# Graph network layer with residual and norm: edge rows fetched in pairs, edge items placed between dense items

## The chip, the cores and the metric

The kernel runs on one core of a Trainium2 chip. The metric is the device time of one execution in microseconds (us). The core has five instruction streams that run in parallel and meet through semaphores: TensorE (PE, with its weight loads listed apart as PEld), VectorE (DVE), ScalarE (ACT), GpSimd (POOL) and SyncE (SP). SP and POOL also issue the DMAs here.

## What is computed

```python
edge_sum = segment_sum(edge_attr, src, num_segments=50000)   # 12500 edges, 128 features
h = elu(concat([x, edge_sum], axis=1) @ W0 + b0)             # x: 50000 x 128, W0: 256 x 128
h = elu(h @ W2 + b2)
out = h @ W3 + b3
result = layernorm(x + out)                                  # over the 128 features
```

All is float32. 12,500 edges name at most 12,500 source rows (11,090 different ones for this input), so most of the 50,000 rows have an edge sum of zero.

## The kernel before

**Dense items.** The 50,000 rows are cut into 98 dense items of 512 rows. A dense item computes its rows as if their edge sum were zero and stores them to `out`. **Edge items.** The edges are sorted by source on the chip (a bitonic network in steps 1 to 19, on DVE with turns on PE). Then 25 edge items of 500 sorted edges each recompute, with the edge sums, the rows that have edges, and scatter them over the dense results in `out`; a last item of 100 rows does the ends of the 100 columns of sorted edges. An edge's row that is not the last one of its source is sent out of bounds and is not written. A scatter must land after the dense store of the same row.

**Steps.** All engines run a software pipeline over steps `c`. In step `c`, PE does `layer1(c-1)`, `turn(c)` for an edge item, `layer2(c-2)` and `layer3(c-3)`, in this order. ACT does `exp(c-1)`, `turned(c)` (x to `xT`), `exp(c-2)`, then `squares(c-3)` with the logarithm and exponential that seed the inverse root. DVE does `root(c-4)`, the first `elu(c-1)`, `normalise(c-4)`, the second `elu(c-2)`. So `h1(c-1)` and `h2(c-2)`, which DVE makes in step `c`, are read by PE in step `c+1`. Each layer's product of 512 columns is two instructions in the trace (they show as x2), and `layer3` is eight pairs of 128 columns.

**The order of items.** Items 0 to 97 are dense, 98 to 122 are the edge items, 123 is `LAST`.

**Edge sums.** For edge group `g`, DVE makes four masks (`masks`, L788) that compare keys, PE multiplies the gathered features by them into `sum_ps` (`sums`, L463), ACT copies the result to `sumT` (`copy_sums`, L574), DVE keeps the edges of it (`keep_parts`, L797), and `layer1` of the edge item adds `w0e` times `sumT` (L498). The step of group `g`'s sums is 95+g. `copy_sums` stands behind `squares` in ACT's step, and the first sum of the next group waits for it (`sum_ready`). At step `END_AT` = 121, `end_sums` puts a short chain PE, DVE, PE, DVE in front of the step.

**Fused bias.** `fused(s, layer)` chooses how the bias gets into a layer. Unfused, DVE uses two instructions for an elu (L819, then L822). Fused, PE adds the bias with a small bf16 product (`add_bias`, L479) and DVE needs one instruction (L815). Steps 3 to 19 are fused in both layers; from step 20 on, only layer 2, and only in even steps of dense items.

**GpSimd.** After the sort it issues, for each group, four gathers of feature rows (L369) and four of x rows (L375), of 125 rows each, paced by `o_ready`; then it waits for all dense stores and issues the 100 scatters (L391) and the last one (L384). Each indirect DMA of 125 rows is one POOL instruction, whose descriptors the engine makes itself.

**SyncE.** In step `c` it issues the load of item `c+3` (L310, 256 KB) and the store of item `c-4` (L317, 256 KB), in order on one queue, and waits for `o_ready` before each store.

## Time and profile before

| | us |
|---|---|
| median of 3 runs | 605.97 (605.18 to 607.83) |
| the profiled execution, its own time | 606.39 |
| its span, first to last instruction | 604.3 |
| PE busy | 544.3 (90%) |
| DVE busy | 466.1 (77%) |
| ACT busy | 439.7 (73%) |
| POOL busy | 371.9 (62%) |

The time of the execution is 2.1 us above the span. The span falls into stages: some 14 us of set-up, the sort with dense items (to step 20, near 101 us), dense items with gathers (to some 400 us), edge items (to some 585 us) and a tail of scatters. An item's steps can be told apart in the timeline by the product of `layer1` (L487), with which each step of PE begins. A timeline row gives start and duration; "x2" merges two instructions; the brackets give the idle time of the engine before it and what ended it. DMA shares are of the core's 16 DMA engines.

### The profile page before, as it was taken

To read this page: it belongs to the slowest core of one execution; us is meant where nothing else is said; L and a number is where in the kernel's file an instruction comes from. 1 tells how busy PE (TensorE), PEld (TensorE's weight loads), DVE (VectorE), ACT (ScalarE), POOL (GpSimd) and SP (SyncE) were. 2 spreads that over 40 slices of the span, in tenths; PEclk is the share of its full clock that TensorE was granted. 3 is DMA by queue.
4 is the path that set the end of the run, shared out by engine and by line. 5 is a ranking of instruction groups with operands and counts; after the bars stand their busy time and mean duration, and the time that the engine had idled before them with its cause. 6 is when DMAs were issued, how large, how long until landed. Compare 5 with 4: busy or idle time off the path is not lost.

```text
span 604.3 us, 10977 instructions
## 1 busy us (share of the span) xinstructions
PE 544.3 (90%) x2930; PEld 360.4 (60%) x2930; DVE 466.1 (77%) x1348; ACT 439.7 (73%) x1632; POOL 371.9 (62%) x310
## 2 busy tenths in 40 slices
PE   3999999999999999999999999989999999997930
PEld 1455555566666666666666666666667666665620
DVE  5988899988888888888888888877678676776640
ACT  2577767888888888888888988876665666665630
POOL 0000000377887787788778778877157777777676
PEclk9999999999999999999999999999999999999985
DMA  3134332486666655555665656554422332211111
GB/s 111 49 109 120 121 106 91 144 245 184 183 180 183 180 175 179 178 174 175 181 180 183 175 174 179 173 153 117 112 77 76 82 79 71 71 38 37 34 39 34
DMA packets 57451, 77.84 MB, mean 129 GB/s; under 512 B 22590, under 2 KB 27782, under 8 KB 57390
## 3 DMA queue, kind: packets, MB, share of 16 engines
q1 hardware_dynamic: 33294, 58.26, 31.7%
q0 software_dynamic: 24096, 18.89, 12.7%
q8 instruction: 24, 0.39, 0.3%
q14 instruction: 37, 0.30, 0.2%
HBM read 45.30 MB, written 32.24 MB: 128 GB/s over the span
## 4 chain that ended last, share of the span: by engine, by line
PE 82%; DVE 9%; issue 5%; POOL 2%; ACT 1%; SPq 0%; DMA 0%; DVEq 0%; POOLq 0%
PE z_ps L531 18%; PE z_ps L532 17%; PE l_ps L519 17%; PE l_ps L487 16%; PE sum_ps L463 5%; PE l_ps L498 4%; PE l_ps L479 3%; PE turn_ps L512 2%; POOL out_dram L391 2%; DVE h L815 2%; DVE net L721 2%; DVE o_sb L850 1%; DVE net L720 1%; PE turn_ps L435 1%; DVE e L819 0%
## 5 line engine op out<-in xcount | busy, mean ns | idle before, releaser
L369 POOL DMA_INDIRECT attr_edge<-in_edge_attr_dram,edge_i x100 | 124.8, 1248 | 143.9 <-issue 141.1
L531 PE MATMUL z_ps<-center,xT 128*128 128x128 f32 (+1 forms) x986 | 194.7, 279 | 8.5 <-issue 6.4
L600 ACT ACTIVATE sq<-z_ps 128x128 f32<-128x128 f32 (+1 forms) x493 | 129.8, 278 | 94.7 <-PE z_ps L532 93.7
L532 PE MATMUL z_ps<-w3c,h 128*128 128x128 f32 (+1 forms) x986 | 190.1, 274 | 0.0
L531 PEld LDWEIGHTS z_ps<-center,xT 128*128 128x128 f32 (+1 forms) x986 | 152.3, 191 | 41.5 <-issue 36.3
L391 POOL DMA_INDIRECT out_dram<-o_sb,target_i x100 | 119.9, 1199 | 53.5 <-issue 49.3
L532 PEld LDWEIGHTS z_ps<-w3c,h 128*128 128x128 f32 (+1 forms) x986 | 149.0, 191 | 0.0
L375 POOL DMA_INDIRECT x_edge<-in_x_dram,key_i x100 | 124.3, 1243 | 30.5 <-issue 28.1
L822 DVE SCALAR_TENSOR_TENSOR h<-l_ps,neg_bias,e 128x512 f32<-128x512 f32 (+2 forms) x174 | 129.2, 742 | 6.2
L519 PE MATMUL l_ps<-h,w 128*128 128x512 f32 (+1 forms) x248 | 130.0, 606 | 1.8 <-DVE h L822 1.8
L591 ACT ACTIVATE e<-l_ps,bias 128x512 f32<-128x512 f32 (+2 forms) x174 | 116.7, 671 | 18.7 <-issue 5.3
L487 PE MATMUL l_ps<-xT,w0x 128*128 128x512 f32 (+1 forms) x248 | 128.8, 601 | 1.2 <-ACT xT L585 1.2
L600 ACT ACTIVATION_READ_ACCUMULATOR sq<-z_ps 128x1 f32 (+1 forms) x493 | 102.0, 207 | 0.0
L819 DVE TENSOR_SCALAR e<-e,bias 128x512 f32<-128x512 f32 (+2 forms) x174 | 95.6, 550 | 3.8 <-issue 2.5
L850 DVE TENSOR_TENSOR o_sb<-z_ps,rstd 128x512 f32<-128x512 f32 (+1 forms) x124 | 84.1, 678 | 0.1
L585 ACT ACTIVATE xT<-x_sb,bias_x 128x512 f32<-128x512 f32 x98 | 69.8, 712 | 7.6 <-DVE neg_bias L668 7.6
L519 PEld LDWEIGHTS l_ps<-h,w 128*128 128x128 f32 x248 | 43.7, 192 | 44.1 <-issue 29.8
L463 PEld LDWEIGHTS sum_ps<-same,attr_edge 125*128 125x128 f32 x200 | 31.8, 190 | 42.9 <-issue 41.7
L832 DVE SCALAR_TENSOR_TENSOR newton<-seed 128x4 f32<-128x4 f32 (+1 forms) x124 | 20.7, 167 | 45.1 <-ACT seed L607 44.3
L591 ACT ACTIVATE e<-l_ps,minus_one 128x512 f32<-128x512 f32 x74 | 49.9, 675 | 4.4 <-PE l_ps L479 3.8
L463 PE MATMUL sum_ps<-same,attr_edge 125*128 125x125 f32 x200 | 39.9, 283 | 12.7 <-issue 12.7
L815 DVE SCALAR_TENSOR_TENSOR h<-e,l_ps 128x512 f32<-128x512 f32 x74 | 50.2, 679 | 0.0
(126 smaller groups left out, 402.5 us busy)
## 6 DMA issues: line engine op xcount, KB each, us to landing
x_sb<-x_items_dram SPq DMA_DIRECT2D x98, 256.0 KB
out_dram<-o_sb SPq DMA_DIRECT2D x98, 256.0 KB
keyB<-key_rows_dram SPq DMA_DIRECT2D x25, 250.0 KB
attr_edge<-in_edge_attr_dram,edge_i POOLq DMA_INDIRECT x100
x_edge<-in_x_dram,key_i POOLq DMA_INDIRECT x100
out_dram<-o_sb,target_i POOLq DMA_INDIRECT x100
w<-in_L_gnn_W_dram SPq DMA_DIRECT2D x2, 64.0 KB, 1.9
w0x<-in_L_gnn_W_dram SPq DMA_DIRECT2D x1, 64.0 KB, 2.1
```

The source lines that it names most:

```text
L369: nc.gpsimd.indirect_dma_start(out=attr_edge[0:EP, c, :], out_offset=None, in_=attr[:, :], in_offset=bass.IndirectOffsetOnAxis(ap=edge_i[0 ...
L375: nc.gpsimd.indirect_dma_start(out=x_edge[0:EP, c, :], out_offset=None, in_=x[:, :], in_offset=bass.IndirectOffsetOnAxis(ap=key_i[0:EP, c: ...
L391: nc.gpsimd.indirect_dma_start(out=out[:, :], out_offset=bass.IndirectOffsetOnAxis(ap=target_i[0:EP, col:col + 1], axis=0), in_=o_sb[0:EP, ...
L463: T.matmul(sum_ps[:, j * EP:(j + 1) * EP], attr_edge[0:EP, c, :], same[0:EP, c % (2 * J), :], start=True, stop=True).then_inc(same_free, 1)
L487: mm = T.matmul(ps, w0x[:], xT[:, c % SLOTS, 0:n], start=True, stop=alone)
L519: mm = T.matmul(l2_ps[c % 2][:, 0:n], w2[:], h1[:, c % 2, 0:n], start=True, stop=not fused(s, 2))
L531: T.matmul(z, xT[:, c % SLOTS, j * q:(j + 1) * q], center[:], start=True, stop=False)
L532: mm = T.matmul(z, h2[:, c % 2, j * q:(j + 1) * q], w3c[:], start=False, stop=True)
L591: A.activation(e[:, c % 2, 0:n], ps[:, 0:n], ACT.Exp, bias=bias[:, 0:1]).then_inc(done, 1)
L600: t = A.activation(sq[0:q, j, :], z_ps[c % 2][0:q, j * P:(j + 1) * P], ACT.Square, scale=float(P) ** -0.5, accum_out=ssq[0:q, c % 2, j:j + 1])
L819: V.tensor_scalar(e[:, c % 2, 0:n], e[:, c % 2, 0:n], 1.0, bias[:, 0:1], ALU.min, ALU.add).then_inc(min_ready, 1)
L822: V.scalar_tensor_tensor(out=h[:, c % 2, 0:n], in0=ps[:, 0:n], scalar=neg_bias[:, 0:1], in1=e[:, c % 2, 0:n], op0=ALU.max, op1=ALU.add).th ...
```

## The change

It has five parts.

1. **Pairs.** A new DRAM tensor `pairs` has a row for each edge: 128 features of its source's x row, 128 edge features. GpSimd fetches x rows by unsorted `src` from the start (100 indirect DMAs, `fetch_x`), SP writes them to `pairs` (25 times `pair_x`, 250 KB, in steps 2 + 3g//2) and copies the features beside them, DRAM to DRAM (25 times `pair_attr`, 256 KB in 512-byte runs, steps 2 to 26). The 200 gathers of 512-byte rows become 100 of 1,024-byte rows.
2. **Order of items.** 50 dense items come first, then edge item, dense, dense, and so on; edge item `g` is item 50+3g, the last is 122. Its sums are in the step before it (49+3g) instead of three steps before. `END_AT` is 123.
3. **Scatter.** DVE derives from the sorted keys how many dense items must be out before group `g` may be scattered (`dense_need`); SP counts landed stores in `dense_out` (`confirm`), and GpSimd waits for that number, read to a register. The scattered rows are written to `pair_edge` instead of `o_sb`.
4. **Sums and their copy.** The four sums stand in two pairs instead of four places, and `copy_sums` stands ahead of `squares`.
5. **Fused bias.** Only steps 3 to 19 are fused; the 40 even steps later are not.

```diff
+    DENSE_BETWEEN = 2
+    ITEMS = [("dense", d) for d in range(ND - DENSE_BETWEEN * (NE - 1))]
+    for g in range(NE):
+        ITEMS.append(("edge", g))
+        if g < NE - 1:
+            ITEMS += [("dense", len(ITEMS) - g - 1 + n) for n in range(DENSE_BETWEEN)]
+    LAST = len(ITEMS)
...
-    SUM_LEAD = 3
-    SUMS = {ND - SUM_LEAD + g: g for g in range(NE)}
+    PAIR_X = {2 + 3 * g // 2: g for g in range(NE)}
+    PAIR_ATTR = {2 + g: g for g in range(NE)}
+    SUM_LEAD = 1
+    SUMS = {EDGE_AT[g] - SUM_LEAD: g for g in range(NE)}
...
         def fused(s, layer):
-            if s < KEY_AT:
-                return FUSED_FROM <= s
-            return layer == 2 and s % 2 == 0 and is_dense(s - 2)
+            return FUSED_FROM <= s < KEY_AT
...
+            def confirm(d):
+                sp.wait_ge(stored[d % SLOTS], 16 * (d // SLOTS + 1))
+                sp.sem_inc(dense_out, 1)
+            def pair_x(g):
+                k = g % SLOTS
+                sp.wait_ge(x_fetched[k], 16 * J * (g // SLOTS + 1))
+                sp.dma_start(pairs.rearrange("(p c) f -> p c f", p=EP)[:, J * g:J * g + J, 0:P],
+                             x_early[0:EP, k, :, :]).then_inc(x_paired[k], 16)
+            def pair_attr(g):
+                last = min(E, ROWS * (g + 1))
+                sp.dma_start(pairs[ROWS * g:last, P:2 * P], attr[ROWS * g:last, :]).then_inc(attr_paired, 16)
...
+                if item_in(c - 4) and is_dense(c - 4):
+                    d = ITEMS[c - 4][1]
+                    store(d)
+                    if d >= 2:
+                        confirm(d - 2)
+                if c in PAIR_ATTR:
+                    pair_attr(PAIR_ATTR[c])
+                if c in PAIR_X:
+                    pair_x(PAIR_X[c])
...
+            def fetch_x(g):
+                k = g % SLOTS
+                at_least(pool, x_paired[k], 16 * (g // SLOTS))
+                for j in range(J):
+                    nc.gpsimd.indirect_dma_start(
+                        out=x_early[0:EP, k, j, :], out_offset=None, in_=x[:, :],
+                        in_offset=bass.IndirectOffsetOnAxis(ap=src_i[0:EP, J * g + j:J * g + j + 1], axis=0),
+                    ).then_inc(x_fetched[k], 16)
...
+            def scatter_out(g):
+                need = pool.value_load(dense_need[0:1, g:g + 1], min_val=2, max_val=ND)
+                pool.wait_ge(o_ready, EDGE_AT[g] + 1)
+                pool.wait_ge(dense_out, need)
...
+            pool.wait_ge(attr_paired, 16 * NE)
             pool.wait_ge(edge_ready, 1)
             for g in range(NE):
                 gather(g)
...
             pool.wait_ge(target_ready, 1)
-            for k in range(SLOTS):
-                pool.wait_ge(stored[k], 16 * DENSE_ON[k])
...
-                return [one(j) for j in range(J)]
+                return [some(0), some(1)]
...
+                if c in SUMS:
+                    parts.append(lambda: copy_sums(SUMS[c]))
                 if item_in(c - 3):
                     parts.append(lambda: squares(c - 3))
                 run(parts, [])
-                if c in SUMS:
-                    copy_sums(SUMS[c])
...
+                link(V.tensor_copy(dense_need[0:1, :], ends[0:1, J - 1:EC:J]))
+                link(V.tensor_scalar(dense_need[0:1, :], dense_need[0:1, :], ROW_BITS, None, ALU.logical_shift_right))
+                V.tensor_scalar(dense_need[0:1, :], dense_need[0:1, :], 2, ND, ALU.add, ALU.min).then_inc(ends_ready, 1)
```

On PE, two dense steps that follow each other in the stage of dense items. `l_ps<-xT,w0x` is layer 1, `l_ps<-h,w` layer 2, `l_ps<-ones_row,bias_rows` the bias product, `z_ps` layer 3. Before:

```order
L487 MATMUL l_ps<-xT,w0x 128x512
L519 MATMUL l_ps<-h,w 128x512
L479 MATMUL l_ps<-ones_row,bias_rows 128x512
L531 MATMUL z_ps<-center,xT 128x128
L532 MATMUL z_ps<-w3c,h 128x128
...
L487 MATMUL l_ps<-xT,w0x 128x512
L519 MATMUL l_ps<-h,w 128x512
L531 MATMUL z_ps<-center,xT 128x128
L532 MATMUL z_ps<-w3c,h 128x128
```

In the changed kernel:

```order
L524 MATMUL l_ps<-xT,w0x 128x512
L556 MATMUL l_ps<-h,w 128x512
L568 MATMUL z_ps<-center,xT 128x128
L569 MATMUL z_ps<-w3c,h 128x128
...
L524 MATMUL l_ps<-xT,w0x 128x512
L556 MATMUL l_ps<-h,w 128x512
```

The bias product of every second step is gone; nothing else of a dense step moved.

On PE, an edge step of before with the sums (`sum_ps`) of a later group in it:

```order
L487 MATMUL l_ps<-xT,w0x 128x500
L498 MATMUL l_ps<-sumT,w0e 128x500
L463 MATMUL sum_ps<-same,attr_edge 128x125
L512 MATMUL turn_ps<-ident,x_edge 128x125 x4
L463 MATMUL sum_ps<-same,attr_edge 128x125
L519 MATMUL l_ps<-h,w 128x500
L463 MATMUL sum_ps<-same,attr_edge 128x125
L531 MATMUL z_ps<-center,xT 125x128
```

In the changed kernel the same work is spread over three steps: the step of the sums, that of the turn and that of the edge item's first layer.

```order
L524 MATMUL l_ps<-xT,w0x 128x512
L500 MATMUL sum_ps<-same,pair_edge 128x125 x2
L556 MATMUL l_ps<-h,w 128x500
L500 MATMUL sum_ps<-same,pair_edge 128x125 x2
...
L524 MATMUL l_ps<-xT,w0x 128x512
L549 MATMUL turn_ps<-ident,pair_edge 128x125 x4
L556 MATMUL l_ps<-h,w 128x512
...
L524 MATMUL l_ps<-xT,w0x 128x500
L535 MATMUL l_ps<-sumT,w0e 128x500
```

The sums now come once in three steps, and two steps lie between them and the product with `w0e`.

On ACT, the copy of the sums. Before, then in the changed kernel:

```order
L591 ACTIVATE e<-l_ps,bias 128x500
L600 ACTIVATE sq,ssq<-z_ps 125x128 x4
L605 ACTIVATE seed<-ssq,eps 125x4
L607 ACTIVATE seed<-seed 125x4
L574 COPY sumT<-sum_ps 128x500
```

```order
L629 ACTIVATE e<-l_ps,bias 128x500
L611 COPY sumT<-sum_ps 128x500
L638 ACTIVATE sq,ssq<-z_ps 128x128 x4
L643 ACTIVATE seed<-ssq,eps 128x4
```

The copy moved from behind the squares of layer 3's result to ahead of them.

## Rows read from the trace of the kernel before

**Rows 1.** Windows view: stretch, then busy us and count of PE, PEld, DVE, ACT, POOL, clock, DMA.

```profile
126.00:390.00 264.00, 258.13 (x1397) 173.37 (x1396) 219.40 (x510) 232.18 (x885) 212.24 (x170) 1.00 0.62 183
```

**Rows 2.** Timeline of two dense steps: start us, us, engine, line, operation, count, [idle <-releaser].

```profile
200.40 1.02 PE L487 MATMUL l_ps<-xT,w0x 128*128 128x512 f32 x2
...
200.60 0.28 ACT L600 ACTIVATE sq<-z_ps 128x128 f32<-128x128 f32 x1 [0.79 <-PE z_ps L532]
...
202.34 0.16 DVE L832 SCALAR_TENSOR_TENSOR newton<-seed 128x4 f32<-128x4 f32 x1 [1.05 <-ACT seed L607]
...
202.92 0.73 DVE L819 TENSOR_SCALAR e<-e,bias 128x512 f32<-128x512 f32 x1
...
203.90 1.02 PE L487 MATMUL l_ps<-xT,w0x 128*128 128x512 f32 x2
...
204.95 0.48 DVE L819 TENSOR_SCALAR e<-e,bias 128x512 f32<-128x512 f32 x1
...
205.46 0.75 DVE L822 SCALAR_TENSOR_TENSOR h<-l_ps,neg_bias,e 128x512 f32<-128x512 f32 x1
...
205.71 0.39 PE L479 MATMUL l_ps<-ones_row,bias_rows 3*128 3x512 bf16 x1
...
206.27 0.49 PE L531 MATMUL z_ps<-center,xT 128*128 128x128 f32 x2 [0.17 <-issue]
...
208.16 1.02 PE L487 MATMUL l_ps<-xT,w0x 128*128 128x512 f32 x2
```

**Rows 3.** Timeline of two edge steps, the first with the sums of a later group.

```profile
474.33 1.01 PE L487 MATMUL l_ps<-xT,w0x 128*128 128x500 f32 x2
...
475.93 0.56 ACT L574 COPY sumT<-sum_ps 128x500 f32<-128x500 f32 x1
...
476.59 0.46 PE L463 MATMUL sum_ps<-same,attr_edge 125*128 125x125 f32 x2 [0.41 <-issue]
...
480.56 1.01 PE L487 MATMUL l_ps<-xT,w0x 128*128 128x500 f32 x2
...
563.96 1.00 PE L487 MATMUL l_ps<-xT,w0x 128*128 128x500 f32 x2
...
568.66 1.00 PE L487 MATMUL l_ps<-xT,w0x 128*128 128x500 f32 x2
```

**Rows 4.** Groups by line and form (busy us, mean ns of one | idle before), and line L834 alone.

```profile
L375 POOL DMA_INDIRECT x_edge<-in_x_dram,key_i x100 | 124.3, 1243 | 30.5 <-issue 28.1 <-DVE o_sb L850 2.4
...
L788 DVE TENSOR_SCALAR same<-keyB,key 125x125 f32<-125x125 f32 x100 | 36.5, 365 | 0.0
...
L834 DVE SCALAR_TENSOR_TENSOR newton<-ssq,newton x124: 159/162/165, 27.2 to 584.3; 128x4 f32<-128x4 f32 x98, 125x4 f32<-125x4 f32 x25, 100x1 f32<-100x1 f32 x1
```

**Rows 5.** DMA: windows of the sort and of the fullest stretch, and the page's two queues.

```profile
30.00:60.00 30.00, 29.53 (x142) 16.11 (x140) 25.07 (x102) 22.26 (x89) 0.00 (x0) 1.00 0.36 111
...
130.00:134.00 4.00, 4.00 (x27) 3.04 (x27) 2.82 (x8) 3.29 (x14) 3.08 (x4) 1.00 1.08 331
...
q1 hardware_dynamic: 33294, 58.26, 31.7%
...
q0 software_dynamic: 24096, 18.89, 12.7%
```

**Rows 6.** Timeline: L487 of step 26, the steps around the end sums, and the tail.

```profile
126.36 1.02 PE L487 MATMUL l_ps<-xT,w0x 128*128 128x512 f32 x2
...
549.36 1.01 PE L487 MATMUL l_ps<-xT,w0x 128*128 128x500 f32 x2
...
557.56 1.03 PE L487 MATMUL l_ps<-xT,w0x 128*128 128x500 f32 x2
...
583.55 0.69 DVE L850 TENSOR_TENSOR o_sb<-z_ps,rstd 125x512 f32<-125x512 f32 x1
...
585.05 1.19 POOL L391 DMA_INDIRECT out_dram<-o_sb,target_i  x1 [0.30 <-DVE o_sb L850]
...
599.98 0.99 POOL L384 DMA_INDIRECT out_dram<-o_sb,end_i  x1 [0.30 <-issue]
```

More of the change, by code:

```diff
@@ L51, in gnn_resnorm @@
     AHEAD = 3
+    DENSE_BETWEEN = 2
[5 more added lines that the diff above has]
+    LAST = len(ITEMS)
+    ITEMS.append(("last", 0))
+    NI = len(ITEMS)
+    DENSE_AT = [c for c in range(NI) if ITEMS[c][0] == "dense"]
+    EDGE_AT = [c for c in range(NI) if ITEMS[c][0] == "edge"]
+    assert [ITEMS[c][1] for c in DENSE_AT] == list(range(ND)) and [ITEMS[c][1] for c in EDGE_AT] == list(range(NE))
     LOG = 7
@@ L260, in blocks @@
             return 1 if c == LAST else J
-        def scatters(c):
-            return 16 * sum(blocks(k) for k in range(ND, c + 1) if k % SLOTS == c % SLOTS)
         def rows(c):
@@ L396, in _ @@
+                        in_=pair_edge[0:EP, c, 0:P], in_offset=None, bounds_check=N - 1, oob_is_err=False,
+                    ).then_inc(scattered, 16)
+            pool.wait_ge(src_loaded, 16)
+            for g in range(NE):
+                fetch_x(g)
+            for k in range(SLOTS):
+                pool.wait_ge(x_paired[k], 16 * len(range(k, NE, SLOTS)))
+            pool.wait_ge(attr_paired, 16 * NE)
             pool.wait_ge(edge_ready, 1)
```

155 lines of the change are left out of this document (72 added, 83 removed).

## The prediction

> **What bounds the kernel now.** I read the windows first, then the timeline step by step, since shares of busy time hide what a step waits for. In the stage of dense items with gathers PE is busy 258 of 264 us, at full clock [rows 1], so PE seems to be the bound and each removed product seems to be worth its length. The timeline says otherwise. Steps begin at 200.40, 203.90 and 208.16: an unfused one of 3.50 us and a fused one of 4.26, 7.76 for two [rows 2]. 3.50 is what PE needs: 2,048 columns (512 for each of two layers, 1,024 in layer 3), or 1.71 ns a column. In the fused step, layer 3 starts at 206.27. The bias product in front of it started at 205.71 and its row ends at 206.10, before that. What ended last was DVE's second elu: 205.46 + 0.75 = 206.21 [rows 2]. So this stage is bound by a loop over two steps: PE ends layer 3 of an item and starts the next step (200.40); ACT, which waits for that, starts the squares at 200.60; DVE starts the root at 202.34, then elu, normalise, elu, and hands over h2 at 206.21; PE starts layer 3 at 206.27 and ends it at 208.16. 0.25 us in it is a DVE instruction that lasted 0.73 instead of 0.48 [rows 2], while GpSimd was making descriptors.
>
> An edge step with sums takes 6.23 us (474.33 to 480.56), one without 4.70 (563.96 to 568.66) [rows 3]. The sums are 4 x 125 columns in float32, 500 x 1.71 ns = 0.86 us. That leaves 0.67 that is no work. ACT's copy of the sums runs from 475.93 to 476.49 and the next group's first sum starts at 476.59 [rows 3]: PE waited for the copy, which stands behind the squares.
>
> At the end, the last edge item is normalised at 583.55 + 0.69 = 584.24, but GpSimd is behind: it issues one scatter in 1.49 us (ten between 585.05 and 599.98) and ends at 600.97, 3.3 us before the end of the span [rows 6].
>
> **Removing the bias products (40 fused steps to none).** By the loop this gives nothing of itself: the unfused step's chain is what both steps wait for, and now every step has it. Two steps take 7.76 - 0.25 = 7.51 without the DVE delay (3.75 each), 7.76 with it in each (3.88). DVE's own work, 202.34 to 206.21 less the 0.25, is about 3.55 a step and fits. The lower bound is PE's 3.50, if ACT or DVE can run ahead, which no row shows; the upper is 3.95, with both elus delayed in some steps. The known delay row is the nearest, but GpSimd's place in the step will drift, so I take two thirds of the delay: 3.83, against 3.88 before. A saving of 40 x 0.76 = 30 us, which the fused step's length suggests, is not there in the dense stage.
>
> **The order of items and the copy of the sums.** From step 49 on, three steps make a cycle: two dense items and one edge item. PE's work is 2 x 3.50 + 4.70 + 0.86 = 12.56 us, in steps of about 4.36 (sums), 3.90 (turn) and 4.30 (product with w0e). Now look at the loop: with the DVE chain of 7.51 over two steps, plus 0.6 for three masks (0.2 each from start to start) where they stand, every two steps here take PE 8.2 to 8.7 us. So in the cycle PE is the bound, the chain is covered, and the fused steps' absence is free. The cover is thin: DVE has 3 x 3.55 + 4 x 0.28 to 0.37 (the masks' mean is 0.365 [rows 4]) + 0.2 = 12.0 to 12.3 of 12.56. The copy is now ahead of the squares, and two steps lie between it and the next sum, so the 0.67 goes; ACT has slack for 0.5 us in a step of 4.3. I take 12.7 a cycle, bounds 12.56 and 13.1. The same three items took 7.76 + 6.23 = 13.99 before: 1.3 saved, 24 times, 31 us.
>
> **Pairs.** GpSimd issues 300 indirect DMAs as before, 1.24 + 0.30 us each [rows 4], but 100 of them from about 3 us on, when it was idle. On SP, `pair_x(g)` waits for a fetch that lands near 12 + 6.2g; SP comes to it near 14 + 7.1g in the sort, and loads and stores queued behind it don't wait. After step 20 SP asks every 5.7 us, but the fetches are up to four groups (25 us) ahead. `pair_x(24)` is in step 38, near 178 us; the gathers then run from 180 to 334, group 0 there by 190 when its sums are due near 216, and each later one 6.2 us after the last, while 12.7 are given. What GpSimd does for `target` and the keys is not touched. The DMA engines are the narrow place. Loads and stores take a share of 0.36 at 111 GB/s in the sort, 0.52 MB in a step of 4.72 us, 1.70 us of all engines [rows 5]. GpSimd's queue moved 18.89 MB in 12.7% of 604.3 us, 4.06 us a MB [rows 5]; at that price three fetches (0.20 MB) are 0.80, two thirds of a `pair_x` 0.68, a `pair_attr` 1.06. The sum is 4.24 of 4.72: it fits, barely. The keys' short DMAs at steps 20 to 24 stand behind such a copy; together with three more DVE instructions I give them 1.0 us (0 to 3).
>
> The Trainium skill (DMA: Bandwidth & Descriptors, Specifications) gives a limit of about 358 GB/s of HBM traffic a core; with both sides of the copy counted this comes to (0.52 + 0.20 + 0.17 + 2 x 0.26) MB in 4.72 us, 299 GB/s, so by that page, as an estimate, it also fits; the fullest stretch of the trace showed 331 GB/s [rows 5].
>
> **Scatters.** They begin at 334 us with some eight items waiting and use 6 us of each cycle's 12.7, so GpSimd is level by about 430. Sources are uniform, so group g needs about 3.9(g+1)+2 dense items, and 50+2g stand before it: only the last two groups wait, group 23 for about a step, group 24 for the last store. Those waits have only scatters behind them.
>
> **The sum, in the trace's own time.** Step 26 begins at 126.4 [rows 6] + 1.0 = 127.4. 23 dense steps x 3.83 = 88.1: 215.5. 24 cycles x 12.7 = 304.8: 520.3. Step 121: 4.36. Step 122: 3.90, and then the end sums, which cost 557.56 - 549.36 - 4.70 = 3.50 [rows 6]: 532.1 for the step of the last edge item's first layer. From there to its normalised rows it was 584.24 - 568.66 = 15.6 [rows 3, 6]; the step behind the end sums was longer by 563.96 - 557.56 - 4.70 = 1.7 [rows 3, 6], and now lies in this stretch: 549.4. GpSimd is level: 0.6 to start, four scatters of 1.49, the last of 0.99, 3.33 to the end: 560.3. Plus 2.1 outside the span, 562.4; the profiled execution stands 0.4 above the median of 605.97: **562.0 us**. Against before, that is 31 in the cycles, 10 in the tail, and little elsewhere.
>
> **The rivals.**
> (a) DVE becomes the bound of the cycle. For: 12.0 to 12.3 of 12.56, and a delay of 0.25 on each of six elus would make 13.5 to 13.8. Against: in steady steps only one in three was delayed. Price 0.5 to 1.1 a cycle: 574 to 588. Chance 0.17.
> (b) The copies hold the sort back. If DRAM to DRAM costs both sides, `pair_attr` is 2.1 and the step needs 5.3 of 4.72: 24 x 0.6 = 14 us, 576. Chance 0.10.
> (c) Slower than before: small packets cost by the piece. SP's queue took 31.7% x 604.3 x 16 / 33,294 = 92 ns a packet, GpSimd's 51 [rows 5]. `pair_attr` and two thirds of `pair_x` put 53 packets of 512 bytes on each engine in a step. At 92 ns a step needs 1.7 + 0.8 + 4.9 = 7.4 us, 24 times 2.7 more: 627. It decides from 76 ns on, where the step takes 1.8 more and the 44 us are gone. GpSimd's rows of 512 bytes speak against it. Chance 0.06.
> (d) The sort's DVE instructions are held by GpSimd, which used to be idle there. Against: L834, with two inputs in SBUF, lasts 165 ns at most in 124 [rows 4], and GpSimd issues DMAs during about 100 of these steps. At 0.3 us for a dozen in each of 15 steps it would cost 54 us: 616. Chance 0.01. The Trainium skill (SBUF — State Buffer, Who interferes with whom) says a VectorE instruction with two SBUF inputs contends with a GpSimd one that reads SBUF; by that rule (d) would come, and the row speaks against it for these DMAs.
> (e) The dense steps run at PE's 3.50: 23 x 0.33 = 8 us less, 554. Chance 0.08.
> (f) The scatters are not level at the end, because `dense_out` comes late: the old tail stays, 572. Chance 0.04.
>
> **How the numbers follow.** The forecast has 0.54, with its own range of 555 to 570 (3.75 to 3.95 a dense step, 12.56 to 13.0 a cycle). 552 to 584 takes in (e), (b), (f) and most of (a), and leaves out (c), (d) and some of the ends, under 0.2. 0.5% is 3 us, about what a measurement can tell here. Faster 0.91, within 0.5% 0.02, slower 0.07.
>
> **What would show it.** Dense steps 26 to 48 at 3.75 to 3.90 with layer 3 behind DVE's elu, not at 3.50; a cycle near 12.7 with PE without gaps; no wait of a sum for the copy; a sort at 4.7 a step; the last scatters within 8 us of the last normalise. Wrong if the DMA share stays at 1 in the sort, or DVE is busy without a gap in the cycle.

## The result, and the profile after

| | before | changed |
|---|---|---|
| median of 20 runs, us | 605.86 (603.84 to 607.87) | 601.5 (591.97 to 605.21) |
| profiled execution, us | 606.39 | 601.51 |
| its span, us | 604.3 | 599.7 |

The ratio changed to before is 0.9837, 95% interval 0.9811 to 0.9863. The forecast was 562.0, with a range of 552 to 584: wrong by 39.5 us. The ratio is taken over each kernel's runs within 1.5% of its fastest, which are 7 of the changed kernel's 20, so it lies under the ratio of the two medians (0.9928). Before's runs lie within 4 us of each other, the changed kernel's within 13. That spread was the first sign that something stood in it that is not in the program.

The engines' busy times and the slices of the page after:

```profile
span 599.7 us, 11136 instructions
PE 534.1 (89%) x2890; PEld 363.3 (61%) x2890; DVE 492.7 (82%) x1391; ACT 434.4 (72%) x1632; POOL 371.2 (62%) x310
PE   3899999779999999999899988788999999999980
ACT  2477775758888888786777774657788887888841
POOL 7766658466672778877887777785444333344306
PEclk9999999989999999999999999989999999999986
```

A slice is 15 us. PE is not full in slices 24 to 28, about 345 to 420 us, at a granted clock of 9 tenths or more but for one slice. The windows view gives the same by stages (stretch, length, then busy us and count of PE, PEld, DVE, ACT, POOL, clock, DMA share, GB/s):

```profile
135.00:224.00 89.00, 83.47 (x459) 57.03 (x458) 80.29 (x185) 78.05 (x299) 57.33 (x46) 1.00 0.76 227
229.00:343.00 114.00, 109.36 (x622) 78.19 (x621) 97.94 (x240) 88.06 (x333) 91.55 (x74) 1.00 0.66 183
343.00:410.00 67.00, 54.45 (x279) 36.25 (x279) 46.13 (x112) 39.99 (x148) 53.49 (x45) 0.97 0.43 118
432.00:560.00 128.00, 127.36 (x749) 93.47 (x749) 113.37 (x293) 106.95 (x401) 48.38 (x40) 1.00 0.38 112
```

From 432 us on PE is busy 127.36 of 128, as forecast for the whole stage. Between 343 and 410 it is busy 54.45 of 67, and so is no one else: DVE 46, ACT 40. DMA has only a share of 0.43 there. GpSimd issues indirect DMAs without a break (45 rows in 67 us): the last gathers, and from 352 us on scatters. The clock explains little: 0.97 instead of 1.00 over 54.45 us of PE's work is some 1.6 us (an estimate from this row).

For the sum I took the start of layer 1 of single items, the rows of L524, item c being in step c+1 (item 25 is the step 26 of the prediction):

```
start of layer 1, us       item 19   item 25   item 48   item 72   item 84   item 96   item 120   end of span
forecast                      -        127.4     215.5      -         -         -       520.3       560.3
changed kernel              101.7      134.6     224.2     333.8     402.6     458.8    560.1       599.7
before                      100.7      126.4       -         -         -         -        -         604.3
```

The 39.4 us that the span is over the forecast are 7.2 up to item 25, 1.5 in the dense steps (89.6 against 88.1), 31.1 in the 24 cycles (335.9 against 304.8) and -0.4 in the tail (39.6 against 40.0). The cycles are not evenly slow: the last eight take 101.3 us, 12.66 each, the forecast's 12.7. The four from item 72 to 84 take 68.8, 17.2 each.

**One slow step, row by row.** The timeline of the changed kernel at 361 to 369 us, ACT first, then PE and GpSimd (start us, us, engine, line, operation, count, [idle before <- releaser]):

```profile
363.51 0.66 ACT L629 ACTIVATE e<-l_ps,bias 128x500 f32<-128x500 f32 x1
364.07 0.71 ACT L623 ACTIVATE xT<-x_sb,bias_x 128x512 f32<-128x512 f32 x1
364.69 0.67 ACT L629 ACTIVATE e<-l_ps,bias 128x512 f32<-128x512 f32 x1
367.92 0.28 ACT L638 ACTIVATE sq<-z_ps 128x128 f32<-128x128 f32 x1 [2.56 <-remote]
...
363.04 0.39 PE L569 MATMUL z_ps<-w3c,h 128*128 128x128 f32 x2
364.84 1.12 PE L524 MATMUL l_ps<-xT,w0x 128*128 128x512 f32 x2 [1.41 <-issue]
...
364.28 1.19 POOL L418 DMA_INDIRECT out_dram<-pair_edge,target_i  x1 [0.30 <-issue]
365.77 1.19 POOL L418 DMA_INDIRECT out_dram<-pair_edge,target_i  x1 [0.30 <-issue]
367.27 1.19 POOL L418 DMA_INDIRECT out_dram<-pair_edge,target_i  x1 [0.30 <-issue]
```

PE ends the last product of z at 363.04 + 0.39 = 363.43. ACT is free at 365.36. It takes up the squares at 367.92, 4.5 us after z was there and 2.56 after it was free itself, and the view names no engine for it ("remote"). The same step on another chip, in the same program (run control2 below):

```profile
364.43 0.68 ACT L629 ACTIVATE e<-l_ps,bias 128x512 f32<-128x512 f32 x1
365.46 0.39 PE L569 MATMUL z_ps<-w3c,h 128*128 128x128 f32 x2
365.88 0.28 ACT L638 ACTIVATE sq<-z_ps 128x128 f32<-128x128 f32 x1 [0.78 <-PE z_ps L569]
365.89 1.19 POOL L418 DMA_INDIRECT out_dram<-pair_edge,target_i  x1 [0.30 <-issue]
```

Here z ends at 365.85 and the squares start at 365.88. GpSimd's scatters are the same.

**TensorE's updates come late.** The trace also records when a semaphore changes. For the step above:

```
update at, us   of                its product's row ended at
361.874         z                 358.50
362.642         layer 1           360.75
367.898         z                 363.43
367.940         layer 1           365.96
367.983         first sum         366.18
374.705         z                 370.83
```

Here PE's results are reported up to 4.5 us after the rows say that they are there (elsewhere in this trace up to 5.4, in that of control below up to 6.1), and then several at once, 42 ns apart. In the run control2 no update of z comes over 0.02 us after its row. (The Trainium skill, TensorE: Matmul & The Clock Gate, The cost: per-tile semaphore tail, says that the increments of matmuls serialize, at about 26 ns each. The 42 ns here are longer than that, and both are small beside the microseconds that are lost.) ACT, which needs z, stands still in the meantime, all that is behind the squares in its list stands too, and PE waits for xT in its turn. In what follows a square is called late when it starts over 0.25 us after both z's row and ACT's own row before it have ended. The profiled run of the changed kernel has 35 late squares, 50.0 us in sum; that of before has 6, 3.5 us.

The 35 are not all among the scatters. GpSimd issues 140 indirect DMAs from 196 to 409 us with no pause of over 0.8 us between two: gathers to 349, scatters from 352. Of the late squares, 5 (6.2 us) fall before 190 us, while x rows are fetched, 14 (13.4 us) between 190 and 343, among the gathers, and 12 (27.2 us) between 343 and 430. The scatters' stretch costs most for its length, but it is not the only one.

### The profile page after: what moved, and what is told of

It is laid out like the page before. It is cut to its first block, busy times and chain, and to the rows that moved or that the text cites. A ratio compares the mean times of both kernels' runs of the same rounds, so it can differ in the third digit from the quotient of the medians.

```text
span 599.7 us, 11136 instructions
## 1 busy us (share of the span) xinstructions
PE 534.1 (89%) x2890; PEld 363.3 (61%) x2890; DVE 492.7 (82%) x1391; ACT 434.4 (72%) x1632; POOL 371.2 (62%) x310
## 4 chain that ended last, share of the span: by engine, by line
PE 57%; DVE 17%; issue 12%; ACT 6%; SPq 3%; another core or an unknown queue 1%; DMA 1%; POOL 1%; POOLq 0%; ACTq 0%; DVEq 0%
PE z_ps L568 13%; PE z_ps L569 13%; PE l_ps L524 11%; PE l_ps L556 11%; DVE e L862 4%; PE sum_ps L500 4%; ACT sq L638 3%; DVE h L865 3%; PE l_ps L535 3%; DVE o_sb L896 1%; PE turn_ps L549 1%; DMA x_sb<-x_items_dram 1%; SPq L323 1%; DVE net L759 1%
## 5 line engine op out<-in xcount | busy, mean ns | idle before, releaser
L418 POOL DMA_INDIRECT out_dram<-pair_edge,target_i x100 | 120.5, 1205 | 122.4 <-issue 106.5
L865 DVE SCALAR_TENSOR_TENSOR h<-l_ps,neg_bias,e 128x512 f32<-128x512 f32 (+1 forms) x214 | 159.1, 744 | 7.6
L397 POOL DMA_INDIRECT x_early<-in_x_dram,src_i x100 | 123.8, 1238 | 58.5 <-DMA pairs_dram<-x_early 28.6
L629 ACT ACTIVATE e<-l_ps,bias 128x512 f32<-128x512 f32 (+1 forms) x214 | 143.4, 670 | 13.4 <-PE l_ps L524 5.3
L407 POOL DMA_INDIRECT pair_edge<-pairs_dram,edge_i x100 | 124.0, 1240 | 42.6 <-issue 30.2
L524 PE MATMUL l_ps<-xT,w0x 128*128 128x512 f32 (+1 forms) x248 | 131.7, 613 | 17.3 <-issue 12.5
L862 DVE TENSOR_SCALAR e<-e,bias 128x512 f32<-128x512 f32 (+1 forms) x214 | 114.8, 536 | 4.5 <-ACT e L629 3.5
L896 DVE TENSOR_TENSOR o_sb<-z_ps,rstd 128x512 f32<-128x512 f32 x98 | 66.7, 681 | 0.1
L524 PEld LDWEIGHTS l_ps<-xT,w0x 128*128 128x128 f32 x248 | 38.7, 196 | 21.9 <-issue 17.4
L500 PE MATMUL sum_ps<-same,pair_edge 125*128 125x125 f32 x200 | 34.7, 283 | 6.5 <-issue 6.1
L643 ACT ACTIVATE seed<-ssq,eps 128x4 f32<-128x4 f32 (+1 forms) x124 | 36.9, 297 | 4.0
```

The source lines that it names most:

```text
L397: nc.gpsimd.indirect_dma_start(out=x_early[0:EP, k, j, :], out_offset=None, in_=x[:, :], in_offset=bass.IndirectOffsetOnAxis(ap=src_i[0:EP ...
L407: nc.gpsimd.indirect_dma_start(out=pair_edge[0:EP, c, :], out_offset=None, in_=pairs[:, :], in_offset=bass.IndirectOffsetOnAxis(ap=edge_i[ ...
L418: nc.gpsimd.indirect_dma_start(out=out[:, :], out_offset=bass.IndirectOffsetOnAxis(ap=target_i[0:EP, c:c + 1], axis=0), in_=pair_edge[0:EP ...
L500: T.matmul(sum_ps[:, j * EP:(j + 1) * EP], pair_edge[0:EP, c, P:2 * P], same[0:EP, c % (2 * J), :], start=True, stop=True).then_inc(same_f ...
L524: mm = T.matmul(ps, w0x[:], xT[:, c % SLOTS, 0:n], start=True, stop=alone)
L629: A.activation(e[:, c % 2, 0:n], ps[:, 0:n], ACT.Exp, bias=bias[:, 0:1]).then_inc(done, 1)
```

## The experiments

Theories at the start: **A**, a row of scatters issued back to back on GpSimd holds TensorE's updates up; **B**, the scatters' data on the way to DRAM does; **C**, any uninterrupted work of GpSimd does, gathers too.

### First chip: alternate, no_scatter, skip_rows, attr_slow

`alternate`, GpSimd's list in another order:

```
-            for g in range(NE):
+            for g in range(8):
                 gather(g)
...
             for g in range(NE):
+                if g + 8 < NE:
+                    gather(g + 8)
                 scatter_out(g)
```

> The changed kernel with GpSimd's list in another order: eight groups of gathers, then one group of gathers and one group of scatters in turn. Every DMA is the same, and no two groups of scatters stand in a row before the last eight. Theory A (a row of scatters issued back to back, as between 343 and 410 us, holds up TensorE's semaphore updates, so that ACT's squares start 2.4 us late in every step there): cycles of 12.8 us from item 48 to item 120 instead of a mean of 14.0, 25 to 31 us less than the changed kernel, about 572 us. Theory B (the scatters' data on the way to DRAM does it): the same bytes are spread over more time, 570 to 585 us. Theory C (GpSimd at work without a pause does it, with gathers or scatters alike): GpSimd now runs without a pause from 180 to about 480 us instead of 430, so no gain, 598 to 612 us.

`no_scatter` drops the loop with `scatter_out`: the edge rows of `out` are left as the dense rows wrote them.

> The changed kernel with the 100 scatters of edge rows left out (the edge rows of the output stay as the dense rows wrote them); the last gather and the last scatter stay. All theories that put the loss after 343 us down to the scatters expect it gone. Theory A: cycles of 12.8 us after 343 us, those before it as they were (13.5 to 14.2 between 282 and 343 us), and a shorter end: 565 to 575 us. Theory C says that the gathers cost about as much in their own stretch (240 to 334 us), 570 to 580 us. If something that has nothing to do with the scatters stretches 343 to 410 us (the loads of x, the clock), the time stays at 592 to 602 us.

`skip_rows`, in `targets()`, so that each target is past the last row and no edge row is written:

```
-  out=target[0:EC, :], in0=dup[0:EC, 2, :], scalar=SKIP, in1=keyA[0:EC, :], op0=ALU.mult, op1=ALU.add)
+  out=target[0:EC, :], in0=dup[0:EC, 2, :], scalar=SKIP, in1=keyA[0:EC, :], op0=ALU.add, op1=ALU.add)
```

> The changed kernel with 65536 added to every target row, so that all 100 scatters are issued as before and every row of them is out of bounds and skipped: GpSimd's work is the same, no edge row is written. Theory A (GpSimd's issue of scatters): steps of 6.0 us and squares 2.4 us late between 343 and 410 us as before, 592 to 605 us. Theory B (the data on its way): this loss is gone, 565 to 575 us.

`attr_slow`:

```
-    PAIR_ATTR = {2 + g: g for g in range(NE)}
+    PAIR_ATTR = {2 + 3 * g // 2: g for g in range(NE)}
```

> The changed kernel with the 25 copies of edge features given out at two in three steps, up to step 38, instead of one a step up to step 26. If transfers crowd the end of the sort (items 19 to 25 took 32.9 us against 25.7 in the kernel before, 8.2 us behind at item 25), item 25 comes 4 to 8 us sooner, and the time is 4 to 8 us under the changed kernel, about 594 us. If GpSimd's gathers of x rows do it, or the wait for the stored words alone, nothing moves: 601 us.

Measured: 568.5, 561.5, 566.6 and 565.4 us, ratios 0.9409 (0.9353 to 0.9465), 0.9264 (0.923 to 0.9298), 0.9377 (0.9352 to 0.9403) and 0.935 (0.9334 to 0.9365). Not one late square in any of the four, 12.62 to 12.72 us a cycle in all. An edit of the sort's copies takes the loss away as well as the edits of the scatters do. Either the program is that fragile or the chip was another one, so these four decide nothing between A, B and C. The expectations of `no_scatter`, `skip_rows` under theory B and `alternate` under A lie near what came, and that is luck here.

### Second chip: after_again, late_copy, fused_dense, no_pairs

`after_again` is the changed kernel itself.

> The changed kernel once more, unaltered, beside the three below. The four runs so far came out at 561 to 568 us whatever they altered, and an experiment that slows the copies of edge features alone took away the loss between 343 and 410 us too. Theory D (the loss between 240 and 420 us, squares late by up to 2.6 us, belongs to the chip or the moment on which the changed kernel was first timed, not to any part of the change): 563 to 570 us now, cycles of 12.8 us throughout. Theory E (each of the four edits breaks up a fragile alignment of GpSimd's issues and TensorE's updates that the changed kernel has by itself): 592 to 605 us again, with late squares in its trace.

It took 577.9 us (573.9 to 582.4), ratio 0.9573 (0.9538 to 0.9609), with 14 late squares (16.3 us) and 14.1 us a cycle from item 72 to 84: between the two theories. The loss depends on the chip. Here 8 of the 14 (11.3 us) come among the backlog of scatters, 6 (4.9 us) while x rows are fetched, and none among the gathers of pairs.

`late_copy`:

```
-                if c in SUMS:
-                    parts.append(lambda: copy_sums(SUMS[c]))
                 if item_in(c - 3):
                     parts.append(lambda: squares(c - 3))
+                if c in SUMS:
+                    parts.append(lambda: copy_sums(SUMS[c]))
```

> The changed kernel with ACT's copy of the sums put back behind the squares, as it stood before. My step in the prediction: the w0e product of the sums' next step then waits, which cost 0.67 us a group in the kernel before. If so, cycles of 13.4 instead of 12.8 us, 24 of them, +12 to +16 us against the changed kernel on the same chip. Rival: in the new order the product has a whole step of its own to wait in, so nothing changes.

581.7 us (579.9 to 589.7). Over the last eight cycles, where neither has more than one late square, it takes 12.83 a cycle against 12.63 of after_again. The place of the copy is worth 0.2 us a cycle, 4 to 5 us in all, a third of what I gave it.

`fused_dense`:

```
-            return FUSED_FROM <= s < KEY_AT
+            if s < KEY_AT:
+                return FUSED_FROM <= s
+            return layer == 2 and s % 2 == 0 and s < EDGE_AT[0]
```

> The changed kernel with the bias of layer 2 added by TensorE in every second dense step after the sort again, as it stood before, up to the first edge item. My step in the prediction: dropping it makes dense steps 3.83 instead of 3.88 us, so putting it back costs 23 x 0.05 = 1 us. Rival: without it VectorE has 0.5 us more work in two steps, and putting it back gains up to 3 us. Item 25 to item 48 is to take 88 to 90 us in the one case and under 87 us in the other.

575.5 us (573.4 to 578.4). Items 25 to 48 take 90.0 us against 90.5. The bias products of layer 2, put back in every second step, cost nothing that can be seen there, as the loop over two steps [rows 2] had said.

`no_pairs`: no `fetch_x`, `pair_x`, `pair_attr`; nine groups of gathers first, then gathers and scatters by turns as in `alternate`; and in `gather(g)`

```
-                        out=pair_edge[0:EP, c, :], out_offset=None, in_=pairs[:, :],
+                        out=pair_edge[0:EP, c, P:2 * P], out_offset=None, in_=attr[:, :],
...
+                        out=pair_edge[0:EP, c, 0:P], out_offset=None, in_=x[:, :],
+                        in_offset=bass.IndirectOffsetOnAxis(ap=key_i[0:EP, c:c + 1], axis=0),
```

> The new order of the items without the pairs: no copy of x rows or edge features to DRAM, GpSimd gathers edge features and x rows separately (200 gathers instead of 100, and no gathers of x rows ahead), nine groups ahead and then a group of gathers and a group of scatters in turn. 300 issues of 1.5 us from about 133 us on are 450 us of GpSimd without a pause, so the end cannot come before 583 us: 586 to 596 us if GpSimd bounds it, with cycles of 18 us for GpSimd beside 12.8 us for TensorE. Item 25 comes at 126.4 us as in the kernel before, if the transfers of the pairs are what held up the sort; at 130 us or more if not. Rival: the extra transfers were never needed, and it takes 560 us.

593.6 us (593.1 to 594.6), ratio 0.9819 (0.98 to 0.9837). Item 120 is reached at 527.0 us, sooner than in the changed kernel on any chip with late squares, but from there to the end it takes 65.8 us, against 38 to 40 in the unaltered changed kernel. Its last rows:

```profile
584.14 1.19 POOL L419 DMA_INDIRECT out_dram<-pair_edge,target_i  x1 [0.30 <-issue]
588.27 1.19 POOL L419 DMA_INDIRECT out_dram<-pair_edge,target_i  x1 [2.95 <-issue]
589.77 0.99 POOL L440 DMA_INDIRECT out_dram<-x_end,end_i  x1 [0.30 <-issue]
```

So the new order without pairs gains 10.7 us on before's 604.3 on this chip, and the changed kernel 26.4. GpSimd's issues bound it (302 in all in both, but here all of them from 112 us on), and the pairs make room by moving 100 of them into the sort. Item 19 comes at 100.7, as in the kernel before, against 101.7 to 103.7 in the four traces of the unaltered changed kernel (103.7 on this chip): the pairs cost 1 to 3 us up to there. Item 25 comes at 130.8, not at 126.4: most of what is lost at the sort's end is lost without any pairs.

This run bears on the theories too. GpSimd issues 219 indirect DMAs from 249 to 584 us, again with no pause of over 0.8 us, and there are only 5 late squares (3.6 us), against 14 in `after_again` on the same chip. Its DMAs come by turns, and its gathers are of 512-byte rows instead of 1,024; which of the two spares it, this run cannot tell.

### Third chip: control, alternate2, skip_rows2, attr_slow2

The unaltered kernel and three of the first four edits side by side.

> The changed kernel unaltered, as the yardstick for the three that follow on the same chip. It has taken 592 to 605 us on the first chip and 574 to 582 us on the second one it was run on, with 38 and 16 steps in which ACT's squares start over 0.25 us after both z and ACT are ready. On a chip without such steps it is to take 563 to 568 us; where they are there, 574 to 605 us.

> Gathers and scatters by turns on GpSimd, as in the run named alternate. If this chip's control is over 573 us: theory A (a backlog of scatters back to back holds up TensorE's updates) has it 8 us or more under the control, without late squares between 343 and 420 us; theory C (any indirect DMAs back to back) has it at or above the control. If the control is at 563 to 568 us, this is the same within 5 us and decides nothing.

> All scatters issued, every row out of bounds and skipped. If the control is over 573 us: theory A (the issue on GpSimd) has this at the control's time with its late squares, theory B (the data of the rows on their way to DRAM) has it 8 us or more under it.

> Copies of edge features at two in three steps up to step 38. If the control has late squares: theory E (a fragile alignment that any edit breaks up) has this without them, at 565 us; if the scatters' backlog makes them, they are here too between 343 and 420 us, and only the sort's end is 1 to 4 us shorter.

| run | us (range) | ratio to before (95%) | late squares, us | a cycle, items 72 to 84 |
|---|---|---|---|---|
| control | 604.6 (596.6 to 614.2) | 0.9893 (0.9853 to 0.9932) | 43, 54.0 | 17.2 |
| alternate2 | 590.6 (584.1 to 595.8) | 0.9756 (0.97 to 0.9812) | 32, 27.2 | 13.1 |
| skip_rows2 | 606.0 (599.3 to 609.1) | 0.9969 (0.9938 to 1.0) | 50, 62.8 | 18.3 |
| attr_slow2 | 604.0 (599.1 to 610.6) | 0.9937 (0.9908 to 0.9966) | 38, 54.0 | 17.9 |

This chip shows the loss, and it tells the theories apart. The waits view of 343 to 410 us (engine, line, waited for: us in total, times, longest), first of control, then of skip_rows2:

```profile
ACT sq L638 <- remote: 20.2, 10, 3.1
PEld l_ps L524 <- issue: 10.1, 8, 2.6
```

```profile
ACT sq L638 <- remote: 24.0, 10, 2.9
POOL out_dram L418 <- issue: 11.9, 39, 0.3
```

With no row written, the squares are as late as ever: **B falls**. It is the issue, not the data. In alternate2 the same stretch reads

```profile
POOL out_dram L418 <- issue: 11.8, 20, 1.9
ACT sq L640 <- PE z_ps L571: 11.3, 11, 1.2
```

with no "remote" among its longest waits; its windows row and control's:

```profile
343.00:410.00 67.00, 65.82 (x377) 47.61 (x376) 59.83 (x147) 53.97 (x203) 49.11 (x41) 1.00 0.57 155
```

```profile
343.00:410.00 67.00, 54.95 (x288) 36.87 (x287) 47.39 (x115) 41.86 (x159) 51.72 (x43) 0.97 0.43 121
```

GpSimd issues 41 instead of 43 DMAs in it, and PE is busy for 65.8 us instead of 55.0. By stretches, the late squares of control and of alternate2 (count, us):

```
                  to 190 us    190 to 343    343 to 430    from 430
control           6,  4.8      19, 21.6      13, 23.0      5, 4.6
alternate2        6,  7.0      12, 10.3       6,  4.3      8, 5.5
```

So the order in which GpSimd issues its DMAs sets the loss, and **A holds** for the part between 343 and 430 us: with the same DMAs by turns, 23.0 us of late squares become 4.3, and the time falls by 14 us by the medians, by 8 by the ratios. Two things it does not tell. By turns there are also only half as many scatters in the stretch, so "scatters in a row" and "each scatter, more than each gather" are not told apart. And a weaker form of C holds besides: control's gathers in a row have 19 late squares with 21.6 us, nearly as much as the scatters, and alternate2 still has 27.2 us of them over the whole run, with cycles of 13.23 on average instead of 12.7. attr_slow2 has the late squares, so it was the chip that made the first four runs fast (theory D, at least for this chip), not the edits (theory E).

### Fourth and fifth chip

> The changed kernel unaltered, the yardstick for the three below on this chip: 563 to 568 us where the trace has no late squares, 574 to 605 us where it has. Two signs are to go together: late squares, and semaphore updates that are missing in the records from 20 us on, when GpSimd begins to issue gathers (on the chip without late squares there is a record of each update; on the two others of six in ten).

control2 took 568.7 us (566.5 to 569.7), ratio 0.9383 (0.9347 to 0.9419), without a late square: the changed kernel, unaltered, 33 us under its first timing. Its span of 567.9 is 133.0 to item 25, 92.8 to item 48, 304.2 in the 24 cycles, 37.9 to the end. 304.2 stands against a forecast of 304.8.

> The 100 scatters left out. If the control is over 573 us: theory A (GpSimd's issue of indirect DMAs holds TensorE's updates back, most where nothing else stands in GpSimd's list) has cycles of 12.6 to 12.8 us from 345 us on, no late squares there, but those of the gathers before 345 us kept; on a chip like that of the run control 575 to 582 us, 22 to 28 us under the control. If the late squares after 345 us stay without scatters, the scatters are not their cause.

560.3 us (558.3 to 566.5), on the same chip: 8 us under control2 by the medians. Of the 11.3 us between the spans, 5.7 lie after item 120, where the last scatters are gone.

> The 100 scatters left out, for the third time, since the first two runs were on chips without late squares. If semaphore updates are missing in this chip's records from 20 us on: theory A has late squares only before 345 us and cycles of 12.6 to 12.8 us after it, 575 to 582 us; if squares are late after 345 us as well, GpSimd's scatters are not what makes them late. If no updates are missing: 557 to 563 us, as twice before.

This third attempt, on the fifth chip, has 7 late squares (9.7 us), all before 160 us while x rows are gathered, none after 345 us, and 12.6 us a cycle from item 72 on; 561.2 us by the median (five of the six runs at 559.1 to 564.4, one at 1880.0). Updates are missing in its records, and for that case I had 575 to 582 us by A: the place of the late squares is as A has it, the time is not, as the 100 gathers in a row have no late square at all here. That this chip can have late squares is seen by the early ones. It fits A that none come late where the scatters were, but without a control on this chip it shows little: how many there would have been with them is not known.

`deeper` moves the squares to item c - 4 and VectorE's root and normalise to c - 5 and the latter ahead of the first elu; the store follows:

```
-                if item_in(c - 3):
-                    parts.append(lambda: squares(c - 3))
+                if item_in(c - 4):
+                    parts.append(lambda: squares(c - 4))
...
-                run([scale, first_layer, output, second_layer], beside)
+                run([scale, output, first_layer, second_layer], beside)
```

> The changed kernel with ACT's squares of an item one step later (at its end, as before, but of the item of four steps ago instead of three), and VectorE's root and normalise one step later at the step's start; the store follows. z then has 3 us until it is read. If what costs is that ACT stands before z at its step's end while TensorE's update is held back, and all else in its list stands behind that, this is 8 to 20 us under a control over 573 us. If the held updates of layers 1 and 2 cost as much, it is within 5 us of the control. On a chip without late squares: within 4 us of the control, or up to 10 us above it if layer 3 has to wait for the later normalise of the item two before.

> Both: squares one step later, and gathers and scatters by turns. If both help by their own way, the fastest on a chip with late squares, 566 to 578 us; on a chip without them 563 to 570 us.

608.5 and 600.0 us, on the chip of control2: a failure, and not where I looked for it. Item 19 comes at 131.5 us instead of 103.3. In the sort the new order has layer 3 wait for the normalise that stands behind sort work; the waits view of deeper at 40 to 100 us:

```profile
DVE net L766 <- PE turn_ps L471: 16.7, 5, 4.9
PE z_ps L568 <- DVE o_sb L896: 13.4, 9, 1.6
```

The last eight cycles kept 12.72. Since the chip had no late squares, the question (where a late update costs) was not answered.

`deeper_alternate` is deeper with alternate, `best_of_both` alternate with attr_slow.

> The changed kernel with gathers and scatters by turns on GpSimd and with the copies of edge features at two in three steps up to step 38. On a chip without late squares 563 to 568 us, like each edit alone. On a chip with them 575 to 592 us: the alternation took 14 us off there, the slower copies nothing that could be told from noise.

570.8 us, ratio 0.9431 (0.9398 to 0.9464), 5.7% under before, with 2 late squares (2.5 us) in its trace; five of its six runs took 568.5 to 572.8 us, one 779.9. No control ran on this chip, so which share of the gain over the changed kernel is the edits' is open. The edit that is shown to help is the alternation: 590.6 us against 604.6 where squares are late, and where they are not, 568.5 on one chip while the changed kernel took 568.7 on another.

### What the records say on the chips

The five groups of experiments ran on five chips, numbered here in their order; which chip the first timing was on is not known. Two counts over traces: how many updates of TensorE, VectorE and ScalarE are on record between 240 and 540 us, of how many that were made; and, while GpSimd issues indirect DMAs without a break, how many of TensorE's recorded updates fall into each 0.3 us of an issue of some 1.5 (issues up to 1.7 us apart; the last column has all from 1.2 on).

```
                          late squares   on record       0-.3  .3-.6  .6-.9  .9-1.2  from 1.2
before (first timing)        6            841 of 1312      73     32     78      0     52
changed (first timing)      35            864 of 1314      27     32     53      7    123
control        chip 3       43            902 of 1303      25     45     50      7    119
skip_rows2     chip 3       50            929 of 1290      39     40     57      4    128
after_again    chip 2       14            946 of 1430      55     43     42     11     84
best_of_both   chip 5        2            980 of 1455      51     36     40      8     82
control2       chip 4        0           1471 of 1472      79     71     66     76     89
attr_slow      chip 1        0           1460 of 1460      77     73     71     89     82
```

On chips 1 and 4 TensorE's updates fall about evenly, and all but one are on record. On the others about a third of all updates in this stretch has no record (28 to 36%), and hardly any of TensorE's is recorded between 0.9 and 1.2 us after an issue begins. Every trace with late squares is of this second kind. The reverse does not hold: before was traced on such a chip too and lost next to nothing, and so did best_of_both. Missing records and late updates may have one cause, or the recording may itself hold the updates up on such chips; no run here was made without recording, which would separate the two.

## Why the prediction was wrong

**The step that failed** is "I take 12.7 a cycle, bounds 12.56 and 13.1" in the part on the order of items. On the chips without late updates it is right to 0.02 (control2 12.68; attr_slow 12.70), and the whole comes near: 568.7 us for the unaltered kernel against 562.0. On the chip of the first timing it was 14.0, which is 31.1 of the 39.4 us missed. What stood in its place: while GpSimd issues indirect DMAs without a break, TensorE's updates reach ACT up to 5.4 us after z is there, and PE waits in its turn. The working took the step from z to squares as it stands in before, where PE goes on to the next step at 200.40 and the squares start at 200.60 [rows 2], and took GpSimd's backlog ("They begin at 334 us with some eight items waiting ... level by about 430") and the gathers ahead of it as work that costs no one else anything. The backlog was there, from 352 to 409 us instead of 334 to 430, and on the third chip its order was shown to set that part of the loss. But an unbroken row of issues is not enough. Before, on a chip with missing records too, issues 201 indirect DMAs from 115 to 425 us and 60 scatters from 443 to 535 without a break, and has 6 late squares. Why it is spared is not settled. Its edge steps of 6.2 us [rows 3] may leave room for an update to be late; its gathers are of 512-byte rows, those of the changed kernel of 1,024. No run tested either.

**T(26), forecast 127.4, came at 134.6.** The forecast gave the sort itself nothing and the keys behind it 1.0 us (0 to 3). Up to item 19 it was 1.0 late (101.7 against 100.7), and 2.2, 2.6 and 3.0 in the other three traces of the unaltered kernel. Items 19 to 25 took 32.9 us against 25.7: 7.2 more, outside the bound. In the same program's other traces they took 27.8, 29.4 and 29.7, so 3 to 5 us of the 7.2 change from run to run and some 2 to 4 do not. The longest step is item 23's, in which DVE works out the ends and `dense_need`: 5.9 us before, 8.9 here, 8.5 in no_pairs. One part lies elsewhere, in the round trip of the sorted words through DRAM. SP's rows of before, and then of after:

```profile
103.60 0.34 SPq L331 DMA_DIRECT2D word_rows_dram<-net  x1
105.32 0.29 SPq L333 DMA_DIRECT2D words<-word_rows_dram  x1
```

```profile
103.29 0.50 SPq L345 DMA_DIRECT2D pairs_dram<-in_edge_attr_dram  x1
104.60 0.35 SPq L359 DMA_DIRECT2D word_rows_dram<-net  x1
108.99 0.30 SPq L361 DMA_DIRECT2D words<-word_rows_dram  x1
```

The small store is issued behind a copy of 256 KB on the same queue, and the read that waits for it comes 4.4 us later instead of 1.7; the key work of PE and DVE waits for that. That the copy in front does it is not shown: with the copies some 5 us ahead (attr_slow) it was 4.5 us, and 2.7 us behind a copy (deeper) 1.8. And no_pairs has the short round trip (1.6) and loses 4.4 us in these items all the same. What that is, is not settled. fused_dense and after_again take 27.6 and 27.8 us for items 19 to 25, so it is not the bias products.

**Dense steps, 3.83 forecast, 3.90 measured** (89.6 in 23): inside the bounds of 3.50 and 3.95, though control2 had 4.03 (92.8), outside them. Putting bias products back changed 0.5 us. That a saving of 30 us "is not there in the dense stage" held.

**The copy of the sums, 0.67 a cycle.** The sign was right, the size not: putting it back cost 0.2. The rest of the way from 13.99 to 12.7 was put down to a loop that PE's work now fills; the cycles of 12.6 to 12.7 with PE busy 127.36 of 128 us fit that, and no run took the parts of it apart.

**Scatters and tail**: GpSimd is level before the end, and the stretch from item 120 took 39.6 us against 40.0. In control2 it took 37.9. The gathers of pairs began at 196 us instead of 180, since the last x rows were in `pairs` only then; the sums waited 0.5 us for them in all.

**The rivals.** (a) DVE as the bound: no, 12.6 to 12.7 a cycle with DVE at 113.37 of 128, 11.2 us a cycle. The prediction gave DVE 12.0 to 12.3, from 3.55 a step; by its own rows (202.34 to 206.21, less 0.25) that is 3.62, which would have left the cover thinner still. (b) and (c) copies or small packets holding the sort back: steps 10 to 19 took 4.79 us against 4.78. (d) GpSimd holding up the sort's DVE work: no, by the same steps; the instruction with two inputs in SBUF, L877 now, lasts 162 ns in the median as before, 232 at most. (e) no, 3.90. (f) no, the tail took 39.6. None of them was the mechanism. What was missing was a rival of the form: an engine that issues DMAs without a break goes with late news of another's results.

## What to carry to other kernels

Time a change on more than one chip before explaining it, always with the unaltered kernel beside it: four different edits "removed" 33 to 40 us here, and one of them, put beside the unaltered kernel on a third chip, gave back nothing (604.0 against 604.6 us). When a busy share falls on all engines at once and the waits name nobody, compare the end of the producer's row with the start of the consumer's; a gap there is time on the way. And where indirect DMAs have piled up on GpSimd beside a stage that TensorE bounds, try them by turns: gathers and scatters by turns took 8 to 14 us less on a chip where it matters, and made no difference that shows where it does not. It is worth a trial and no rule, as the kernel before had longer rows of them at hardly any cost.

## What the runs showed of the hardware

- On four of the six chips or timings, some of TensorE's semaphore updates came late, up to 6.1 us after z's row ended (control), while GpSimd issued indirect DMAs, and hardly any was recorded between 0.9 and 1.2 us after an issue began (7 of 246 in control, 76 of 381 in control2). On the two others z's update came within 0.02 us of its row's end throughout.
- Scatters of which every row is skipped go with as many late squares as real ones (50 against 43).
- An unbroken row of issues alone is not enough: before issued 201 indirect DMAs in a row and had 6 late squares in its trace, 3.5 us.
- The same program took 568.7, 577.9 and 604.6 us on three chips, while the kernel before took 605.4, 604.3 and 607.0 beside it.
- No trace whose records are complete had a late square; every one that had them lacks records, most of them about a third between 240 and 540 us. Whether a run of which no updates are recorded would have them late, no run here can tell.
- The round trip of the sorted words over SP's queue and DRAM, from the issue of a store of 50 KB to that of the read that waits for it, took 3.1 to 5.5 us in 16 traces with the pairs' copies, but 1.8 in two others with them (deeper, deeper_alternate), and 1.6 and 1.7 in the two without (no_pairs, before).
